# A linear attention loop in three overlapped stages, with its masked products multiplied in two 64-column halves

## The reference

```python
qkv = einsum('btd,ed->bte', x, w_qkv)            # 16 heads of 8
q, k = rope(q), rope(k)
q_phi, k_phi = elu(q) + 1, elu(k) + 1
kv_prefix = cumsum(k_phi[..., :, None] * v[..., None, :], axis=1)
k_prefix = cumsum(k_phi, axis=1)
num = einsum('bthd,bthdm->bthm', q_phi, kv_prefix)
denom = sum(q_phi * k_prefix, axis=-1)
attn = (num / (denom + 1e-6)) @ w_o.T
delta = x - shift_by_one_row(x)
x = x + sigmoid(delta @ w_gate.T + b_gate) * attn
```

## Time and profile before

| | |
|---|---|
| median of 3 runs (lowest to highest) | 5664.89 us (5663.38 to 5672.79) |
| the profiled execution's own time | 5666.5 us |
| its span, first to last instruction | 5664.7 us |
| granted TensorE clock, mean over the span | 0.925 of 2.4 GHz |
| TensorE, VectorE, ScalarE busy | 4998.0, 4058.9, 3784.5 us |
| first and last instruction of the loop | 95.4 and 550.9 us |

### The profile page before, as it was taken

The page is one execution under the profiler, slowest core; times in us unless marked ns, Lnnn a source line. Parts: engine busy times, 40 slices in busy tenths (PEclk is TensorE's granted clock), DMA queues, the critical chain, the costliest instruction groups (busy, mean ns, idle before and its releaser), DMA issues. The chain is left out here.

```text
span 5664.7 us, 146153 instructions
## 1 busy us (share of the span) xinstructions
PE 4998.0 (88%) x41236; PEld 4163.6 (74%) x41236; DVE 4058.9 (72%) x11142; ACT 3784.5 (67%) x12309; POOL 2454.7 (43%) x3763
## 2 busy tenths in 40 slices
PE   5997895999259998899979999899988999899994
PEld 3665684899248887788868887688877888688873
DVE  4544475777758887788868887688876888688875
ACT  1111342443149997799959998699977999599982
POOL 0000000000246664566636666466655666366661
PEclk7877796999679999999999999999999999899997
DMA  0000110000111111111111111111111111111111
GB/s 20 0 0 15 37 37 1 0 0 0 30 28 25 25 25 47 30 25 25 25 50 25 25 25 49 28 25 25 25 46 28 25 25 25 49 28 25 25 45 31
DMA packets 103075, 144.80 MB, mean 26 GB/s; under 512 B 65245, under 2 KB 72690, under 8 KB 102386
## 3 DMA queue, kind: packets, MB, share of 16 engines
q1 hardware_dynamic: 93410, 107.27, 8.4%
q0 software_dynamic: 9232, 33.12, 1.9%
HBM read 49.13 MB, written 2.10 MB: 9 GB/s over the span
## 5 line engine op out<-in xcount | busy, mean ns | idle before, releaser
L1912 ACT ACTIVATE d_probs<-d_S_ps,d_neg_max 128x96 f32<-128x96 f32 x3072 | 1002.9, 342 | 59.3 <-issue 47.0
L1513 POOL TENSOR_TENSOR d_qk<-d_qk,d_sin_terms 128x512 f32<-128x512 f32 x768 | 961.0, 1273 | 30.5 <-DVE d_sin_terms L2099 30.5
L1688 PEld LDWEIGHTS d_S_ps<-d_kT,d_q_blocks 128*128 128x128 f32 x6144 | 789.5, 192 | 2.2
L1688 PE MATMUL d_S_ps<-d_kT,d_q_blocks 128*128 128x96 f32 x6144 | 788.9, 271 | 0.0
L2099 DVE TENSOR_TENSOR d_qk<-d_A_ps,d_tables 128x512 f32<-128x512 f32 x768 | 527.9, 687 | 236.1 <-ACT d_squares L1868 168.9
L1912 ACT ACTIVATION_READ_ACCUMULATOR d_probs<-d_S_ps,d_neg_max 128x1 f32 x3072 | 638.5, 208 | 0.0
L1645 PE MATMUL d_A_ps<-d_wqkv_hi,d_xT_hi 128*128 128x512 f32 x1152 | 558.8, 485 | 19.5 <-DVE d_sin_terms L2099 14.8
L1868 ACT ACTIVATE d_squares<-d_A_ps 128x512 f32<-128x512 f32 x768 | 462.4, 602 | 127.1 <-PE d_A_ps L1647 126.8
L2099 DVE TENSOR_TENSOR d_sin_terms<-d_A_ps,d_tables 128x512 f32<-128x512 f32 x768 | 523.1, 681 | 0.0
L1920 ACT ACTIVATE d_probsT<-d_PT_ps 96x512 f32<-96x512 f32 (+1 forms) x768 | 460.4, 600 | 80.4 <-PE d_PT_ps L1698 80.4
L1652 PE MATMUL d_T_ps<-d_ident,d_qk 128*128 128x128 f32 x3072 | 482.2, 280 | 33.6 <-POOL d_qk L1550 29.1
(11 more groups left out here) (406 smaller groups left out, 10977.9 us busy)
## 6 DMA issues: line engine op xcount, KB each, us to landing
d_v_early<-d_v SPq DMA_DIRECT2D x192, 256.0 KB, 2.9
d_v_early<-d_v SPq DMA_DIRECT2D x192, 128.0 KB, 2.3
d_tables<-L_ffn_rotary POOLq DMA_DIRECT2D x7, 2048.0 KB, 8.3
d_qk<-L_ffn_Wqkv POOLq DMA_DIRECT2D x21, 512.0 KB, 4.0
d_xs<-d_xb SPq DMA_DIRECT2D x56, 127.0 KB
d_xs<-d_xb SPq DMA_DIRECT2D x96, 63.5 KB
ax_fp_blocks<-L_ffn_blocks_gu SPq DMA_DIRECT2D x16, 256.0 KB, 3.9
ax_fp_scales<-L_ffn_scales_gu SPq DMA_DIRECT2D x64, 64.0 KB, 3.5
```

Of the source, the lines that this page charges most:

```text
L1513: nc.gpsimd.tensor_tensor(c4[:, :, s, :], c4[:, :, s, :], s4[:, :, 1 - s, :], ALU.add).then_inc(rotated, 1)
L1688: last = nc.tensor.matmul(S[g % 2][:, n * SEEN:(n + 1) * SEEN], qx[:, p, half, :], kT[b][jj][:, p, HALF * half:HALF * half + SEEN], start= ...
L1912: nc.scalar.activation(pr[:, g, n, seen_columns(g)], S[g % 2][:, n * SEEN:(n + 1) * SEEN], ACT.Exp, bias=nmax[:, g, n:n + 1], accum_out=de ...
```

## The change

The loop is written as a software pipeline over steps u = 0 to 31. Step u computes the products of tile u, finishes tile u - 1 (its last three groups of numerators, its output transpose, projection and gate) and starts tile u + 1 (projections, rotation, `phi`). Four things come with it. Each numerator matmul is split in two, with 64 weight columns each, which write the lower and the upper half of the partitions. The masked queries `qx` are made by ScalarE in four copies with a scale from memory, where VectorE made them in one instruction. The output's transpose goes to the bank `o` instead of `T`. The state's update has a buffer for each sequence, and a new semaphore `state_read` lets VectorE add it while later work runs. The number of products, their size and the masks are as before.

```diff
+                    def numerators(u, b, g):
+                        pe.wait_ge(masked, u * 4 + (g + 3))
+                        for h in range(4 * g, 4 * g + 4):
+                            for half in range(2):
+                                rows = slice(64 * half, 64 * half + 64)
+                                last = nc.tensor.matmul(num_b[rows, h * VW:(h + 1) * VW], pr[:, g, h % 4, rows],
                                                         va[:, b, h * VW:(h + 1) * VW], start=False, stop=True,
                                                         skip_group_check=True)
-                        last.then_inc(num_ps, 1)
+                        if g == 3:
+                            last.then_inc(num_ps, 1)
...
+                    def products(u, b, g):
+                        pe.wait_ge(qx_ready, u * 4 + 4)
                         pe.wait_ge(kx_ready, u * 4 + 4)
...
+                    def step(u, b, first=False, last=False):
+                        if not first:
+                            numerators(u - 1, 1 - b, 1)
+                        if not last:
+                            project_qk(u + 1, 1 - b)
+                        transpose_phi(u, b, first)
+                        if not first:
+                            numerators(u - 1, 1 - b, 2)
+                            numerators(u - 1, 1 - b, 3)
+                        update(u, b)
+                        products(u, b, 0)
+                        if not last:
+                            project_v(u + 1, 1 - b)
+                        products(u, b, 1)
+                        if not last:
+                            project_gate(u + 1, 1 - b)
+                        if not first:
+                            transpose_attn(u - 1)
+                        products(u, b, 2)
+                        if not first:
+                            project_out(u - 1)
+                        from_state(u, b)
+                        numerators(u, b, 0)
+                        products(u, b, 3)
```

On ScalarE:

```diff
+                    def copy_q_heads(u, b):
                         act.wait_ge(qkT_ps, u + 1)
...
+                        for h in range(4):
+                            nc.scalar.activation(qx[:, b, h, :], T_b[:, 0:P], ACT.Identity, scale=head4[:, h:h + 1]
+                                                 ).then_inc(qx_ready, 1)
...
+                    def step(u, b, first=False, last=False):
+                        gate_tanh(u, b)
+                        copy_q_heads(u, b)
+                        copy_k(u, b)
+                        if not first:
+                            copy_attn(u - 1)
+                        if not last:
+                            copy_v(u + 1, 1 - b)
+                        copy_q(u, b)
+                        if not last:
+                            exps(u + 1, 1 - b)
```

On VectorE:

```diff
-                        nc.vector.tensor_tensor(qx[:, b], T_b[:, 0:P].unsqueeze(1).broadcast_to([P, 4, P]),
-                                                head4[:].unsqueeze(2).broadcast_to([P, 4, P]), ALU.mult).then_inc(qx_ready, 1)
...
+                    def step(u, j1, b, first=False, last=False):
+                        if not last:
+                            cosines(u + 1, j1, 1 - b)
+                        if not first:
+                            denominators(u - 1)
+                        if not last:
+                            sines(u + 1, j1, 1 - b, 0)
+                        if not first:
+                            inverses(u - 1)
+                        if not last:
+                            sines(u + 1, j1, 1 - b, 1)
+                        if not first:
+                            attention(u - 1)
+                        mask_products(u, 0)
+                        if not last:
+                            rotated_sum(u + 1, 1 - b)
+                        mask_products(u, 1)
+                        if not last:
+                            negatives(u + 1, 1 - b)
+                        mask_products(u, 2)
+                        if not first:
+                            gate(u - 1, 1 - b)
+                        if not last:
+                            phis(u + 1, 1 - b)
+                        if not first:
+                            add_update(u - 1, 1 - b)
+                        mask_update(u, b)
+                        mask_products(u, 3)
+                        if not first:
+                            add_gated(u - 1)
```

More of the change, by code:

```diff
@@ L720, in tile, with from_state @@
                         last.then_inc(qkT_ps, 1)
-                        if more:
-                            project(u + 1, 1 - b)
-                        pe.wait_ge(qx_ready, u + 1)
+                    def products(u, b, g):
+                        pe.wait_ge(qx_ready, u * 4 + 4)
                         pe.wait_ge(kx_ready, u * 4 + 4)
[L726 to L729, removed]
+                        pe.wait_ge(masked, u * 4 + (g + 1))
+                        nc.tensor.matmul(s_b[g % 2][:], kx[:, b, g, :], qx[:, b].rearrange("p h t -> p (h t)"),
+                                         start=True, stop=True).then_inc(s_ps, 1)
+                    def from_state(u, b):
                         pe.wait_ge(qT_ready, u + 1)
@@ L733, in tile, with update @@
                         pe.wait_ge(state_ready, u + 1)
-                        nc.tensor.matmul(num_b[:, 0:W], qT[:, b, :], state[:, b, :], start=True, stop=True)
+                        nc.tensor.matmul(num_b[:, 0:W], qT[:, b, :], state[:, b, :], start=True, stop=True).then_inc(state_read, 1)
+                    def update(u, b):
                         pe.wait_ge(v_ready, u + 2)
@@ L748, in tile, with project_out @@
+                    def project_out(u):
                         pe.wait_ge(aT_ready, u + 1)
-                        pe.wait_ge(gated, u + 2)
                         nc.tensor.matmul(o_b[:, 0:D], aT[:], wo[:], start=True, stop=True).then_inc(o_ps, 1)
[L752 to L756, removed]
+                    def step(u, b, first=False, last=False):
[22 more added lines that the diff above has]
+                        products(u, b, 3)
@@ new lines, in _ @@
+                    project_qk(0, 0)
+                    project_v(0, 0)
+                    project_gate(0, 0)
+                    step(0, 0, first=True)
+                    with pe.Fori(0, STEPS // 2 - 1) as i:
+                        for par in range(2):
+                            step(i * 2 + (1 + par), 1 - par)
+                    step(STEPS - 1, 1, last=True)
+                    for g in range(1, 4):
+                        numerators(STEPS - 1, 1, g)
+                    transpose_attn(STEPS - 1)
@@ L758, in _ @@
+                    project_out(STEPS - 1)
                 @block.scalar
@@ L861, in tile @@
                         nc.vector.scalar_tensor_tensor(row, gt[:], 0.5, row, ALU.mult, ALU.add).then_inc(x2_ready, 1)
-                    with v.Fori(0, J - 1) as j:
-                        for b in range(B):
-                            tile(j, b)
-                    tile(J - 1, 0)
-                    tile(J - 1, 1, more=False)
+                    def step(u, j1, b, first=False, last=False):
[26 more added lines that the diff above has]
+                        mask_products(u, 3)
+                        if not first:
+                            add_gated(u - 1)
@@ new lines, in _ @@
+                    cosines(0, 0, 0)
+                    sines(0, 0, 0, 0)
+                    sines(0, 0, 0, 1)
+                    rotated_sum(0, 0)
+                    negatives(0, 0)
+                    phis(0, 0)
+                    step(0, 0, 0, first=True)
+                    with v.Fori(0, STEPS // 2 - 1) as i:
+                        for par in range(2):
+                            step(i * 2 + (1 + par), i + 1, 1 - par)
+                    step(STEPS - 1, J - 1, 1, last=True)
@@ L870, in conv_attention_mixture @@
+                    denominators(STEPS - 1)
+                    inverses(STEPS - 1)
+                    attention(STEPS - 1)
+                    gate(STEPS - 1, 1)
+                    add_gated(STEPS - 1)
         with ExitStack() as c1:
```

110 lines of the change are left out of this document (60 added, 50 removed).

## The result

The changed kernel takes 5525.57 us (median of 4 runs, 5523.19 to 5526.97) against 5667.73 for the kernel before in the same comparison. The ratio is 0.9748, with a 95% interval of 0.9732 to 0.9765. The profiled execution took 5523.19, with a span of 5521.5, so the span is 143 us shorter than before. One of the four executions of the kernel of experiment 10 took 7527.29 us at a mean granted clock of 0.587, and that experiment's figures are those of the other three.

The account below looks back on a forecast made before the run. TensorE, at mean clock 0.78, was taken to set the loop's time. 31 x (14.04 - 10.9) + 3.8 = 101 us off 5666.5 gave 5565.5, and a median 1.6 below, 5564 us; range 5528 to 5622, 84%.

Parts of the forecast that it names:

- 2.66 + 7.16 = 9.8 us: One loop step at full clock: 2.66 from second transpose to first product, 7.16 for the rest on TensorE.
- The path of 2.66 from transposes to first product: Second transpose to first product: 0.32 until ScalarE starts, 4 x 0.25 query copies, 1.15 for kx, 0.2 until product.
- TensorE waits for some 1.0 us in each step: Before the first product: TensorE's work covers about 1.6 of the 2.66 us ScalarE path, and nothing hides the rest.
- Numerators: Split records in the loop: 0.71 us per group of 16, 1.18 for two groups, 2.6 a step against some 3.5.
- Four copies with one scale from memory: Masked queries on ScalarE: 0.25 us per copy, between bounds of 0.16 and 0.34.
- The end: From the last transposes to the kernel's end: 13.0 us instead of 15.7.
- the clock's term: Over the loop: half-clock share falls from 44% to 19%, making a step 10.9 us instead of 9.8.
- nothing else changes: Outside the loop: later work depends on the loop only by its end, so the kernel saves what a tile saves.
- A: Rival for the loop: the clock never falls, 135 us less, 5530 us; chance 15%.
- B: Rival for the loop: half clock keeps its 44% share or similar waits appear, 12.6 us a step, 5617 us; chance 19%.
- C: Rival for the loop: stages do not overlap, only numerators gain, 0.9 to 1.0 us a tile, 5635 us; chance 7%.
- D: Rival for the numerators: a record keeps its 0.11 us price whatever its columns, 117 us more, 5782 us; chance 5%.

Follow-up runs that it names:

- experiment 10: The changed kernel with the masked queries back on VectorE in one multiplication, ScalarE's qT copy waiting for it: median 5547.9 us, ratio 0.9779.
- experiment 8: The changed kernel, but each product waits only for its own key group's ScalarE copy, not all four: median 5489.1 us, ratio 0.9669.
- experiment 9: The changed kernel with one unused 384-column matmul per step filling the wait before the first product: median 5511.8 us, ratio 0.9714.
- experiment 5: The kernel before with 20 tiny unused ScalarE copies ahead of the linear attention loop: median 5648.6 us, ratio 0.9952.
- experiment 2: The kernel before with only the numerators split into two halves of 64 weight columns, old schedule kept: median 5618.5 us, ratio 0.9914.
- experiment 1: The changed kernel without the split, each numerator one matmul of 128 weight columns again: median 5539.1 us, ratio 0.9768.
- experiment 12: The kernel of experiment 11 without the split, each numerator one matmul of 128 weight columns: median 5581.4 us, ratio 0.9829.
- experiment 11: The kernel of experiment 8 with all four numerator groups in one row behind the transposes of phi: median 5465.2 us, ratio 0.9632.

## Why the prediction was wrong

The direction and the working of the step were right; two steps failed, both to the same side.

**What held.** "So a step is 2.66 + 7.16 = 9.8 us with the full clock throughout": 9.89. The path of 2.66 from transposes to first product: 2.69. "TensorE waits for some 1.0 us in each step": 0.94, and experiment 8 gave back that and more. Numerators: 0.71 for a group of 16 was 0.66 from neighbour to neighbour, and 1.18 for 32 was 1.13, counted in the same way. Four copies with one scale from memory: (1.14 - 0.37) / 3 = 0.26 apart, taken as 0.25. The Trainium skill, "ScalarE: Activation LUTs", What ACT_TABLE_LOAD costs, adds 93 ns for each such operand. An estimate from that page's figure and the 0.16 without one is 0.25, and the trace agrees with 0.26. The buffers, waits and the other bank cost nothing that the step shows. The end takes 12.2, predicted 13.0. In one place the prediction's arithmetic slips: by its own sum, steps of 10.2 to 11.7 us give 5542 to 5589, not 5538 to 5587.

**The first failed step: the clock's term.** "I scale the 44% with the length: 44% x 4.0/9.3 = 19% of the time. A step is then 9.8/(1 - 0.095) = 10.9." The direction was right, the size not: the share was 12% (clock 0.94) and the step 10.33, so that the term of 1.1 us a step measured 0.44 over the 9.89. A mean of 10.9 would have needed a fall in two steps of three; it came in one of four, at some 1.4 each. This is 31 x 0.57 = 18 us. Scaling the share by the length of the stretch had no row behind it, and the runs show falls as events of single steps, at one step in four or at none: experiments 8 and 9 removed a gap of 0.94 us in two ways, and the falls behind the start went with it both times. Inside this term lies a smaller miss the other way: step 0 was to be 1.1 us shorter than the others, and took 12.2.

**The second failed step: nothing else changes.** "Nothing after the loop depends on it but by its end, so what a tile saves, the kernel saves." The windowed part took 23 us less, and ScalarE's waits at its jumps 24 less in sum. Experiment 5 gave 25 less in those waits and 15 less in the windowed part from moved code alone, with the old loop. Experiment 10 took 16 of the 24 back with a shorter ScalarE program. That the stall changes with what stands in ScalarE's program 1.5 ms earlier is shown. That it is the place of the later code that counts is the likeliest reading: the copies also bring a spare tile, but experiment 10 changes the stall without one, and experiment 2, which lengthens TensorE's program alone, doesn't change it. Why the place should matter isn't shown. With these, 101 + 18 + 24 = 143 us.

**The rivals.** A (the clock never falls, 5530) was nearest to the total, but by luck: seven steps behind the start do have falls, and the 24 us outside the loop, of which it knew nothing, made up for them. B and C did not come. D, a price of 0.11 for each record whatever its columns, is refuted in the loop itself: 32 records of 64 weight columns take 1.10, and 32 of 128 take 3.64, with the same 9 moving columns. The Trainium skill, "TensorEngine Tiling (Array Packing)", Instruction Overhead, gives each matmul an overhead of about 60 cycles and names no weight columns. An estimate from that page's figure is 0.025 us at 2.4 GHz. The trace agrees with it for 64 weight columns (0.03), but not for 128, where a record takes 0.11. So the page's figure is not D's price. Its advice against a tiling factor from a small dimension, which the prediction took as one against this split, doesn't reach it either: the factor comes from the 128 weight columns.

**Where the gain comes from.** Schedule alone 110, split alone 52, both 119, each known to some 10 us, since the loop before takes 444 to 461 in four runs. What the split is worth depends on what stands over it: 8 us where a wait for ScalarE hides most of the longer row (experiment 1), 52 in the old order, 120 where nothing hides it and the clock falls too (experiment 12). The move of the queries to ScalarE is worth nothing in the loop (experiment 10).

**Open.** Why ScalarE's stall at the jump depends on its code's place, and whether the windowed part's gain of some 20 us is exactly this stall's: equal kernels differ there by some 8 us. Why the first steps of experiment 8 take 14.8 and 11.7. What decides how often the clock falls: behind the first two steps there were no falls with 0 and 0.16 us idle before the first product (experiments 8 and 9), three with 0.38 (experiment 1), eleven with 0.66 (experiment 10) and seven with 0.94 (the kernel after), and nearly every step had one in experiment 12 without any idle time. So idle time alone doesn't order them.

## What to carry to other kernels

Before a price is put on an edit, ask what covers the place: the same split gave 8, 52 and 120 us in three orders of the same work, and a one-word change of a wait gave another 38 once the overlap stood. Where an engine's program changes length, compare the stalls at the jumps of later loops as well; 24 of these 143 us were outside the loop, beside stalls that were shorter by as much, and a comparison of totals alone would have put them down to the loop. Sum a step at the full clock first and treat falls of the clock as events of a step, with a range that reaches beyond none at all on the fast side, since other parts of the kernel can gain too.

## What the runs showed of the hardware

- ScalarE's stall where a hardware loop jumps back had a median of 1.03 us, 0.73 with ten instructions more in its program 1.5 ms earlier, and 0.30 with twenty. In the kernel after it was 0.35, and 0.37 with twenty more: a floor of about 0.3.
- At clock 1.0 an fp32 matmul with 9 moving columns took 0.11 us a record with 128 weight columns (3.64 for 32, experiment 12), and 0.03 with 64 in pairs of halves (2.04 for 64, experiment 11).
- TensorE can be busy for 99% of a loop and still be at clock 0.78 (experiment 12), where rows of 32 such records of 128 weight columns stand in it; with the 64-column pairs in the same place it was at 0.97 (experiment 11). And with 0.94 us of idle time in a step of 9.89 us the kernel after had a fall in every fourth step; with that time filled, or taken out, there was none behind the first two (experiments 9 and 8).
